# A fused state-space block and quantised MLP: TensorE's and ScalarE's order within a block redone, four convolution taps packed into three products

## What is computed

```python
# first recurrence, 64 states
conv = conv_b + sum(x_pad[k:k+L] * conv_w[k])            # the condition row is the filter's tap pair
B, C = softplus(conv @ Wp[:, :64] + ..), tanh(conv @ Wp[:, 64:] + ..)
state = decay * state + dt * B * (x @ Ws + bs);  y0 = C * state
r = y0 @ Wo + bo
# Mamba block on r
xn = layernorm(r);  xz = xn @ W_in;  x_br, z = split(xz)
xb = silu(causal_conv4(x_br) + conv_b)                   # 1024 channels, 4 taps
Bm, Cm = xb @ W_b, xb @ W_c;  delta = softplus(xb @ W_delta + b_delta)
h = exp(delta * A) * h + delta * Bm * xb                 # 1024 channels x 16 states
y = sum(h * Cm) + xb * Dp
x2 = x + r + (y * silu(z)) @ W_out
# a low-rank layer made from the condition, then a ternary-weight MLP with int8 rows and gelu
out = x2 + bitlinear(gelu(bitlinear(x2 + x2 @ layer)))
```

## Time and profile before

| | us |
|---|---|
| median of 3 runs (2626.81 to 2627.16) | 2627.09 |
| the profiled execution | 2629.67 |
| its span | 2627.8 |
| VectorE busy | 2267.9 (86%) |
| TensorE busy | 2300.7 (88%) |
| ScalarE busy | 1669.8 (64%) |
| GpSimd busy | 1725.5 (66%) |
| one block (steps 1 to 14) | 126.1 |

### The profile page before, as it was taken

How to read it: one execution, slowest core, us unless ns; L and a number is a source line. 1 busy time by engine, 2 the same in 40 slices (tenths; PEclk the granted TensorE clock), 3 DMA queues, 4 the chain that set the end, 5 groups by cost and what they waited for, 6 DMA issues and landing times. The chain is left out here.

```text
span 2627.8 us, 34242 instructions
## 1 busy us (share of the span) xinstructions
PE 2300.7 (88%) x11488; PEld 1587.1 (60%) x11520; DVE 2267.9 (86%) x2248; ACT 1669.8 (64%) x3372; POOL 1725.5 (66%) x2041
## 2 busy tenths in 40 slices
PE   7778888888888989898888888989898978999997
PEld 5556666666666666666675757666666433444443
DVE  2399999999999999999999999999999874888886
ACT  2566676767676676767676667676667753555554
POOL 0287787878787878787877878787878732222221
PEclk8889999999999999999999999999998997999999
DMA  4102020202020101111010202020114522111110
GB/s 188 73 1 73 9 73 10 77 5 77 5 81 16 67 18 65 33 49 57 25 65 17 73 10 73 10 72 10 65 41 165 204 84 95 65 63 60 60 53 25
DMA packets 48299, 151.74 MB, mean 58 GB/s; under 512 B 8069, under 2 KB 8965, under 8 KB 45198
## 3 DMA queue, kind: packets, MB, share of 16 engines
q1 hardware_dynamic: 48142, 149.76, 16.0%
HBM read 132.37 MB, written 17.37 MB: 57 GB/s over the span
## 5 line engine op out<-in xcount | busy, mean ns | idle before, releaser
L489 POOL TENSOR_TENSOR ring<-ring,Crows 128x512 f32<-128x512 f32 x1024 | 1281.5, 1272 | 44.6 <-POOL carry L482 0.4
L925 DVE TENSOR_TENSOR_SCAN ring<-a_ps,ring 128x1024 f32<-128x1024 f32 x512 | 1167.6, 2281 | 106.1 <-ACT a_ps L744 104.7
L744 ACT ACTIVATE a_ps<-delta,nA 128x255 f32<-128x255 f32 x2048 | 850.0, 466 | 366.9 <-DVE ring L925 365.9
L1138 PE MATMUL yT_ps<-ident,ring 128*128 128x128 f32 x4096 | 585.2, 284 | 170.2 <-POOL ring L489 167.8
L1138 PEld LDWEIGHTS yT_ps<-ident,ring 128*128 128x128 f32 x4096 | 474.4, 144 | 289.1 <-POOL ring L489 249.1
L917 DVE TENSOR_TENSOR ring<-u_ps,Brows 128x1024 f32<-128x1024 f32 x512 | 619.6, 1210 | 22.3 <-PE yT_ps L1138 15.4
L1104 PE MATMUL work<-xb,big 128*128 128x256 f32 x2048 | 474.0, 383 | 10.0 <-ACT zs L577 10.0
L1104 PEld LDWEIGHTS work<-xb,big 128*128 128x128 f32 x2048 | 384.1, 192 | 80.2 <-issue 18.4
L482 POOL TENSOR_TENSOR carry<-ring,half 128x4 f32<-128x4 f32 x512 | 126.2, 246 | 366.0 <-DVE ring L925 364.3
L1375 POOL TENSOR_TENSOR m<-m,pows 128x1 f32<-128x1 f32 x64 | 34.1, 547 | 324.6 <-DVE m L1526 324.6
L1120 PE MATMUL work<-Wout,xb 128*128 128x512 f32 x512 | 243.8, 612 | 0.0
(11 more groups left out here) (199 smaller groups left out, 2531.4 us busy)
## 6 DMA issues: line engine op xcount, KB each, us to landing
Brows<-bc_rows SPq DMA_DIRECT2D x64, 512.0 KB, 4.5
Crows<-bc_rows SPq DMA_DIRECT2D x64, 512.0 KB, 3.7
xT<-in_xT SPq DMA_DIRECT2D x16, 514.0 KB, 3.6
x_rows<-x2row SPq DMA_DIRECT2D x32, 256.0 KB, 2.0
xp<-x_rows SPq DMA_DIRECT2D x32, 256.0 KB, 2.7
xx<-in_x SPq DMA_DIRECT2D x32, 256.0 KB, 2.9
out_rows<-orow SPq DMA_DIRECT2D x32, 256.0 KB, 2.0
delta<-in_c_w SPq DMA_DIRECT2D x6, 1024.0 KB, 5.2
```

What stands on the lines that cost most here:

```text
L489: nc.gpsimd.tensor_tensor(hp, hp, Cbc[:, G * g + GP * c:G * g + GP * c + GP, :], ALU.mult)\
L744: r = nc.scalar.activation(a_ps[q % 2][:, i, 1:T], delta[:, par, dt, 1:T], ACT.Exp, scale=nA[:, dt, s:s + 1])
L925: dve.tensor_tensor_scan(ring[:, q % RING, :, :].rearrange("p g t -> p (g t)"), a_ps[q % 2][:, :, :].rearrange("p g t -> p (g t)"), ring[: ...
L1138: r = pe.matmul(yT_ps[:, tt, :], ring[:, q % RING, i, P * tt:P * tt + P], ident[:, :], is_transpose=True, start=False, stop=(g == NG - 1 a ...
```

## The change

**TensorE's order.** GT3's transposes move from slot 3 to slot 2, wout from slots 4 to 9 into 3 to 8. x runs in slots 10 to 14 for 10 to 15. z(0) moves from 19 to 16, z(1) from 21 to 22, z(2) and z(3) from 25 and 26 to 27 and 28; delta's pieces close up, with dl(2, .) done by slot 27. `BANK` is changed to match (Z1 to bank 0, Z2 and Z3 to bank 1).

**ScalarE's order.** `prj` (Exp alone) is in slot 4, `prj_ln` in 5 without a load. A new `visit` in slot 5 loads the Silu set, runs Tanh and z's silu of the block being scanned, and loads the Exp and Ln set again; z's silu leaves slot 30. `dexp(0)` moves from 25 to 23, `dexp(1)` from 27 to 26, `dtail` and `dln` both to 27, `zcopy` from 21, 23, 27, 28 to 18, 24, 28, 29. `gT(3)` moves from 6 to 4, `wout(0)` from 9 to 8. The copy `keep_y0` comes over from VectorE. VectorE's `gates0` moves from slot 4 to 3.

**Packed taps.** Taps 0 and 1 of the 64 states fill one product of 128 rows, fed by `yp` (y0 and y0 shifted by one, one above the other). Their bias and ones rows ride in rows 96 and 97 of the products of taps 2 and 3. So a piece has three products for four. `y0back` makes `yp` and the rows 96 and 97 with three more copies before it hands over. z then reads 66 rows.

**Last step.** Two of the weight scales (`SCALE`) move from slot 0 to slot 7.

```diff
 BANK = {"PRJ": 0, "GT3": 1, "WOUT0": 1, "WO0": 0, "WO1": 0, "WOUT1": 1, "YT": 0, "YB": 0, "GT0": 1,
-        "XB0": 0, "XB1": 1, "XB2": 0, "XB3": 1, "BC": 0, "GT1": 1, "Z0": 1, "Z1": 1, "DL0": 0,
-        "DL1": 1, "Z2": 0, "Z3": 0, "GT2": 1, "DL2": 0, "DL3": 1}
+        "XB0": 0, "XB1": 1, "XB2": 0, "XB3": 1, "Z0": 1, "BC": 0, "GT1": 1, "DL0": 0, "Z1": 0, "DL1": 1,
+        "DL2": 0, "GT2": 1, "Z2": 1, "Z3": 1, "DL3": 1}
...
-        SCALE = {0: range(0, 4), 7: range(4, 12), 9: range(12, 16)}
+        SCALE = {0: range(0, 2), 7: range(2, 12), 9: range(12, 16)}
...
+                def visit():
+                    nc.scalar.preload_act_table_set("silu_and_others")
+                    if front:
+                        nc.scalar.activation(c0[:, :], work[BANK["PRJ"]][N0:P, 0:T], ACT.Tanh, bias=sc0[N0:P, 4:5])\
+                            .then_inc(s_tanh, 1)
+                    if scan:
+                        zsilu(k, par)
+                    nc.scalar.preload_act_table_set("natural_log_exp_and_others")
...
-                    act.wait_ge(s_yh, n + 1)
-                    nc.scalar.activation(y0s[0:NY, fp, 3:T + 3], ps[0:NY, 0:T], ACT.Copy).then_inc(free[BANK["YB"]], 1)
+                    act.wait_ge(s_yh, 2 * n + 1)
+                    nc.scalar.activation(y0s[0:NY, fp, 3:T + 3], ps[0:NY, 0:T], ACT.Copy).then_inc(s_yh, 1)
+                    act.wait_ge(s_yh, 2 * n + 2)
+                    nc.scalar.activation(yp[0:N0, :], y0s[0:N0, fp, 0:T], ACT.Copy)
+                    nc.scalar.activation(yp[N0:2 * N0, :], y0s[0:N0, fp, 1:T + 1], ACT.Copy)
+                    nc.scalar.activation(y0s[CROW:CROW + 2, fp, 2:T + 3], y0s[N0:NY, fp, 0:T + 1], ACT.Copy)\
+                        .then_inc(free[BANK["YB"]], 1)
...
-                next_plan = {5: [prj], 6: [prj_ln], 8: [lambda: stats(0)], 9: [lambda: stats(1)], 10: [y0scale],
-                             11: [y0back], 14: [lambda: xcopy(0)], 15: [lambda: xcopy(1)], 16: [lambda: xcopy(2)],
-                             17: [lambda: xcopy(3), silu], 20: [bc], 21: [lambda: zcopy(0)], 23: [lambda: zcopy(1)],
-                             25: [lambda: dexp(0, False)], 27: [lambda: zcopy(2), lambda: dexp(1, False), lambda: dtail(0, False)],
-                             28: [lambda: zcopy(3), lambda: dln(0, False)], 30: [lambda: zsilu(n, fp)],
-                             31: [lambda: dexp(2, False)]}
+                next_plan = {4: [prj], 5: [prj_ln], 8: [lambda: stats(0)], 9: [lambda: stats(1)], 10: [y0scale],
+                             11: [y0back], 13: [keep_y0], 14: [lambda: xcopy(0)], 15: [lambda: xcopy(1)],
+                             16: [lambda: xcopy(2)], 17: [lambda: xcopy(3), silu], 18: [lambda: zcopy(0)],
+                             20: [bc], 23: [lambda: dexp(0, False)], 24: [lambda: zcopy(1)],
+                             26: [lambda: dexp(1, False)], 27: [lambda: dtail(0, False), lambda: dln(0, False)],
+                             28: [lambda: zcopy(2)], 29: [lambda: zcopy(3)], 31: [lambda: dexp(2, False)]}
...
-                back_plan = {6: [lambda: gT(ND // 2 - 1, fp)], 9: [lambda: wout(0)], 12: [lambda: wout(1)]}
+                back_plan = {4: [lambda: gT(ND // 2 - 1, fp)], 8: [lambda: wout(0)], 12: [lambda: wout(1)]}
...
-                next_plan = {4: [gates0], 5: [scan0], 13: [keep_y0]}
+                next_plan = {3: [gates0], 5: [scan0]}
...
-                    for tap in range(4):
-                        r = pe.matmul(ps[:, T * m:T * m + T], Mx[:, tap, c:c + P], y0s[:, fp, tap:tap + T],
-                                      start=(tap == 0), stop=(tap == 3))
+                    for i, rows in enumerate((yp[:, :], y0s[:, fp, 2:T + 2], y0s[:, fp, 3:T + 3])):
+                        r = pe.matmul(ps[:, T * m:T * m + T], Mx[:, i, c:c + P], rows, start=(i == 0), stop=(i == 2))
...
-                plan = {0: [("n", prj, 0)], 1: [("n", prj, 1)], 2: [("n", prj, 2)],
-                        3: [("b", turn_gated, ND // 2 - 1, k - 1)], 4: [("b", wout, 0, 0)],
...
-                        17: [("n", bc)], 18: [("s", turn_gated, 1, k)],
-                        19: [("n", z, 0), ("n", dl, 0, 0)], 20: [("n", dl, 0, 1)],
...
+                plan = {0: [("n", prj, 0)], 1: [("n", prj, 1)], 2: [("n", prj, 2), ("b", turn_gated, ND // 2 - 1, k - 1)],
+                        3: [("b", wout, 0, 0)], 4: [("b", wout, 0, 1)],
+                        5: [("n", wo, 0), ("b", wout, 0, 2)], 6: [("n", wo, 1), ("b", wout, 1, 0)],
+                        7: [("n", turn_y0), ("b", wout, 1, 1)], 8: [("b", wout, 1, 2)], 9: [("n", turn_back)],
+                        10: [("n", x, 0, 0), ("n", x, 0, 1)], 11: [("s", turn_gated, 0, k), ("n", x, 1, 0)],
+                        12: [("n", x, 1, 1), ("n", x, 2, 0)], 13: [("n", x, 2, 1), ("n", x, 3, 0)], 14: [("n", x, 3, 1)],
+                        16: [("n", z, 0)], 17: [("n", bc)], 18: [("s", turn_gated, 1, k)],
+                        19: [("n", dl, 0, 0), ("n", dl, 0, 1)], 20: [("n", dl, 0, 2), ("n", dl, 0, 3)],
+                        21: [("n", dl, 1, 0)], 22: [("n", z, 1), ("n", dl, 1, 1)], 23: [("n", dl, 1, 2)],
+                        24: [("n", dl, 1, 3), ("n", dl, 2, 0)], 25: [("n", dl, 2, 1)],
+                        26: [("s", turn_gated, 2, k), ("n", dl, 2, 2)], 27: [("n", dl, 2, 3), ("n", z, 2)],
+                        28: [("n", z, 3)], 29: [("n", dl, 3, 0), ("n", dl, 3, 1)],
+                        30: [("n", dl, 3, 2)], 31: [("n", dl, 3, 3)]}
```

More of the change, by code:

```diff
@@ L516, in prj, with keep_y0 @@
                         act.wait_ge(s_setD, 8)
+                    wait(act, s_c0, 6 * n)
                     nc.scalar.activation(e0[:, :], ps[0:N0, 0:T], ACT.Exp, bias=sc0[0:N0, 4:5]).then_inc(s_e0, 1)
-                    wait(act, s_c0, 6 * n)
-                    nc.scalar.activation(c0[:, :], ps[N0:P, 0:T], ACT.Tanh, bias=sc0[N0:P, 4:5]).then_inc(s_tanh, 1)
                 def prj_ln():
-                    nc.scalar.preload_act_table_set("natural_log_exp_and_others")
                     act.wait_ge(s_c0, 6 * n + 1)
                     nc.scalar.activation(e0[:, :], e0[:, :], ACT.Ln, bias=1.0).then_inc(s_l0, 1)
+                def visit():
[6 more added lines that the diff above has]
+                    nc.scalar.preload_act_table_set("natural_log_exp_and_others")
+                def keep_y0():
+                    if back:
+                        act.wait_ge(full[BANK["WOUT1"]], jobs_before("WOUT1", k) + 1)
+                    act.wait_ge(s_c0, 6 * n + 5)
+                    nc.scalar.activation(y0k[:, fp, :], y0[:, :], ACT.Copy).then_inc(s_c0, 1)
                 def wout(tt):
@@ L715, in step @@
                         job()
+                    if q == 5 and (front or scan):
+                        visit()
                     if scan and q in turned:
@@ L814, in scan0 @@
                     dve.memset(mark[:, :], 0.0).then_inc(free[BANK["PRJ"]], 1)
-                def keep_y0():
-                    if back:
-                        dve.wait_ge(full[BANK["WOUT1"]], jobs_before("WOUT1", k) + 1)
-                    dve.wait_ge(s_c0, 6 * n + 5)
-                    dve.tensor_copy(y0k[:, fp, :], y0[:, :]).then_inc(s_c0, 1)
                 def mx_scale():
+                    dve.wait_ge(s_mtz, 1)
                     for m in range(ND):
@@ L1064, in turn_m @@
                             pe.wait_ge(s_mxc, m - 1)
-                        for tap in range(4):
-                            r = pe.transpose(abank[2 + m % 2][0:NY, P * tap:P * tap + P], MTk[:, m, tap, :], ident[:, :])
+                        for i in range(3):
+                            r = pe.transpose(abank[2 + m % 2][:, P * i:P * i + P], MTk[:, m, i, :], ident[:, :])
                         r.then_inc(s_mxp, 1)
```

40 lines of the change are left out of this document (17 added, 23 removed).

## The result

The changed kernel takes **2570.65 us** (2569.67 to 2572.65) against 2627.12 (2626.81 to 2629.68): a ratio of 0.978, 95% between 0.9768 and 0.9793. The forecast was 2549 in a range of 2526 to 2588: inside, with 56 us won where 78 were forecast. The span went from 2627.8 to 2569.5.

The account below looks back on a forecast made before the run. VectorE sets the pace. Per block -4.3 us, so -60 for fourteen blocks; with head -12, the rest of step 0 -3.7 and tail -2, 78 off the median 2627.09 gives 2549, range 2526 to 2588.

Parts of the forecast that it names:

- Part 1, slot 5: ScalarE's visit in slot 5 hides behind VectorE's recurrence with 2.1 us to spare; the 0.58 wait goes.
- Part 1, gates0: VectorE's clip, moved to slot 3, waits for the Exp: 0.3 us a block taken, between 0 and 0.95.
- Part 2: The copy of y0 leaves VectorE for ScalarE's slot 13: gain 0.27 us a block.
- Parts 3 and 4: Packed x saves TensorE 3.5 us; XB3 is full 5.8 earlier, so slot 17's 3.60 wait goes, 0.8 to spare.
- Part 5: Slots 24 to 31: old waits go, new ones of 3.15 us come in slots 26 to 29; net +0.1 a block.
- Part 6: Ring-buffer waits in slots 9 and 11 fall from 0.6 to about 0.35 us: -0.25 a block.
- Head: Steps -1 and 0: waits of 11.6 us for softplus products shrink to about 1.3; -12 us, between -6 and -14.
- Step 0: The rest of step 0, taken as a block without the Ln: -3.7 us.
- The rival of the dips: End of block late or TensorE dipping to 1.2 GHz in gaps: 2.35 us a block, 2582; chance 0.12.
- Its prj part: A clock dip at prj, costing 0.65 us more a block.
- Its other part: A clock dip in slots 24 to 28, costing 1.7 us a block.

Follow-up runs that it names:

- e5_zfirst_prjfirst: The changed kernel with z(0) moved ahead of slot 15's state transposes and prj's first part ahead of slot 31's; 2529.91 us.
- e4_unpack: The changed kernel with the packing alone undone: four products for a piece of x, one copy of y0's rows for four; 2598.76 us.
- e8_packonly: The kernel before with the packing alone: three products a piece of x and three more copies in y0back; 2590.26 us.
- e1_warm: The changed kernel with four extra products on TensorE in slot 16, ahead of slot 15's state transposes, the result unchanged; 2554.9 us.
- e11_z3early: The kernel of e5_zfirst_prjfirst with z(2) ahead of DL2's last quarter and z(3) at the end of slot 27; 2531.89 us.

## Why the prediction was right, and 22 us off

The span by stretch, from the first recurrence of one block (slot 5 in both kernels) to the next: head -9.7 (forecast -12), step 0's block -0.4 (-3.7), thirteen blocks -41.7 (-55.9), the rest -6.5 (-6.3).

- **Part 1, slot 5: right.** No wait; slot 5's exponentials end 2.5 before VectorE wants them, 2.1 was forecast. Four loads a block, each 1.28; no drain beside them shows.
- **Part 1, gates0: the term was mis-sized.** 0.3 was taken, 0.86 measured (mean over the thirteen blocks), and the clip itself 0.40 for 0.26. The size was that of prj at full clock, without the dip; the wait is 1.3 to 1.9 behind the dip, above the 0.95 that the text gave as its upper end. e5_zfirst_prjfirst removes it.
- **Part 2: right** where it can be read (0.26 for 0.27).
- **Parts 3 and 4: right.** x's last product ends 0.8 ahead of ScalarE's copy, as forecast, and slot 17 waits for nothing. e4_unpack (0.5 to 0.8) and e8_packonly (1.00) show that neither the order nor the packing alone does it.
- **Part 5: right in the net,** 2.60 of waits for the forecast 3.15 and 2.63 before. But the first product of a block was to stay at 1.75 and took 0.67 in all but one block (0.76): 0.99 a block that I did not count. That is luck. Over the run it is 14.9 us (58.1 for 43.2 of `u`), without which the time would be about 2585, near the end of the range.
- **Part 6: right** as far as it went, 0.2 for 0.6. **The step that failed** is what it leaves out: it looked for ring waits in slots 9 and 11 only. Slot 19 has 1.67 in the mean.
- **Head: inside its bounds,** one wait of 2.22 for three, where 1.3 was counted; gates0 and its clip cost another 1.6 in step 0. **Step 0:** its -3.7 were lost to 2.34 in slot 19 and to a wait of 1.86 and a clip of 1.19 at gates0; in e1_warm, without the first and with 0.29 at gates0, the block is 5.3 shorter than before.

Per block: -0.58 (slot 5) + 0.86 + 0.14 (gates0) - 0.27 - 3.60 - 0.03 - 0.42 + 1.67 - 0.99 = -3.22, measured -3.21.

The rival of the dips, at 0.12, was the mechanism, together with the order that puts z(0) ahead of bc; it named the gaps in slots 15 and 16 and beside the last scan. Its prj part came near its price, 0.56 too much for 0.65, and 0.14 in the clip. Its other part was placed in slots 24 to 28, where the clock is 0.98 to 1.00 in every block; it belonged to slots 15 to 17, where I had the gap in the text and no price for what runs behind it. The Trainium skill, "TensorE: Matmul & The Clock Gate", Part 1, which makes the half clock the default that activity lifts, agrees with e1_warm: 1.7 us of idle work gave 16 us back.

## What to carry to other kernels

When a change thins an engine's work, follow its list through the gaps that appear and price what runs right behind each gap at the lower clock; here moving two ready jobs into two gaps won 41 us on top of the change's 56. A long job is free only where its engine has a lead: z's silu showed no wait in slot 5, where it shares its table loads, and cost 51 us in slot 30, where load, silu and load take 4.6. And a wait taken away shows up at the next late thing until the whole chain moves: slot 28, 29, gates0, and only then the time.

## What the hardware showed unexpectedly

- One and the same block comes mostly in two lengths, 122.1 and 123.6, in turns, and the clock goes with them: in the changed kernel prj's 16 records take 3.6 or 4.2 to 4.8, bc's 4.6 to 6.2. Why they take turns stays open.
- VectorE's clip of 64 x 256 takes 0.26 alone and up to 1.4 (e11_z3early) beside a product of GpSimd; the product of 128 x 510 takes 0.67, or 1.2 to 1.8 when it starts behind one, and where the first of a block took 0.67, GpSimd's pair took 2.98 for 2.50. The Trainium skill, "SBUF — State Buffer", section "Who interferes with whom", says that VectorE, in an instruction with two inputs in SBUF or in a two-port mode, shares a pair of ports with GpSimd, and that the one that issues first keeps the other out until it is done; these durations agree. A list that shifts by a microsecond can change who comes first, and no wait shows it.
